# Second attention's output projection in fp16 halves with a power-of-two scale of its own for each chunk, and a new order of the loop

## The reference

```python
def attn_b(x, ...):                       # the second attention
    ...                                   # q, k turned by position, projected to rank 16, gated
    def step(M, inp):
        q_t, k_t, v_t, g_t = inp
        M = M * decay + einsum('bhr,bhd->bhrd', g_t * k_t * scale, v_t)
        y = einsum('bhr,bhrd->bhd', q_t, M)
        return (M, y)
    ...
    out = Y @ out_w.T + out_b             # what this change is about: 512 x 512
    hres = x + out
    ...                                   # layer norm of hres, times ln_g, plus ln_b

x = x + attn_a(layernorm(x), ...)
x = x + ffn(layernorm(x), rhs)
x = x + attn_b(layernorm(x), ...)
x = x + ffn(layernorm(x), rhs)
```

## Time and profile before

| | |
|---|---|
| median of 3 runs | 3149.44 us |
| the profiled execution's own time | 3152.03 us |
| its span, first to last instruction | 3150.2 us |
| TensorE busy | 3027.0 us (96%) |
| VectorE busy | 2457.6 us (78%) |
| GpSimd busy | 1028.1 us (33%) |
| ScalarE busy | 734.0 us (23%) |
| mean granted TensorE clock | 0.983 of full speed |
| DMA | 153.89 MB, 49 GB/s |

### The profile page before, as it was taken

The page is one execution under the profiler, slowest core; times in us unless marked ns, Lnnn a source line. Parts: engine busy times, 40 slices in busy tenths (PEclk is TensorE's granted clock), DMA queues, the critical chain, the costliest instruction groups (busy, mean ns, idle before and its releaser), DMA issues.

```text
span 3150.2 us, 126598 instructions
## 1 busy us (share of the span) xinstructions
PE 3027.0 (96%) x54932; PEld 2288.7 (73%) x54932; DVE 2457.6 (78%) x5410; ACT 734.0 (23%) x1357; POOL 1028.1 (33%) x1398
## 2 busy tenths in 40 slices
PE   3699999999999999999999999999999999999995
PEld 3477777777777777777777777777777777777763
DVE  7777787787787887787787778778778778778774
ACT  2222221222222222222122122222222222222211
POOL 2023333333333333333333333333333333333332
PEclk9799999999999999999999999999999999999997
DMA  5222222222222222222222222222222222222220
GB/s 176 62 40 50 42 45 50 42 45 51 41 45 51 41 49 47 44 47 49 44 48 45 45 47 45 51 41 45 51 41 47 49 42 48 49 46 45 48 41 20
DMA packets 384395, 153.89 MB, mean 49 GB/s; under 512 B 352801, under 2 KB 361633, under 8 KB 383905
## 3 DMA queue, kind: packets, MB, share of 16 engines
q1 hardware_dynamic: 383904, 146.02, 23.4%
HBM read 45.29 MB, written 16.78 MB: 20 GB/s over the span
## 4 chain that ended last, share of the span: by engine, by line
PE 94%; DVE 3%; issue 1%; DMA 1%; ACT 0%; POOL 0%; POOLq 0%; SPq 0%; DVEq 0%; ACTq 0%
PE bank L726 22%; PE bank L727 21%; PE bank L728 21%; PE bank L1020 7%; PE bank L899 3%; PE bank L808 3%; PE bank L852 3%; PE bank L684 3%; PE bank L972 2%; PE bank L871 2%; PE bank L826 2%; PE bank L995 2%; PE bank L982 1%; DVE absmax L1163 1%; PE bank L1008 1%
## 5 line engine op out<-in xcount | busy, mean ns | idle before, releaser
L726 PE MATMUL bank<-xaT,wq_hi 128*128 128x128 f16 x2048 | 362.5, 221 | 4.5 <-DVE absall L1173 4.5
L726 PE MATMUL bank<-xbT,wb 128*128 128x128 f16 x2048 | 350.8, 220 | 13.3 <-DMA xbT<-work 13.3
L727 PE MATMUL bank<-xaT,wq_hi 128*128 128x128 f16 x2048 | 361.1, 221 | 0.0
L728 PE MATMUL bank<-xaT,wq_lo 128*128 128x128 f16 x2048 | 361.0, 221 | 0.0
L726 PE MATMUL bank<-xaT,wk_hi 128*128 128x128 f16 x2048 | 358.5, 220 | 0.0
L727 PE MATMUL bank<-xaT,wk_hi 128*128 128x128 f16 x2048 | 358.4, 220 | 0.0
L728 PE MATMUL bank<-xaT,wk_lo 128*128 128x128 f16 x2048 | 358.4, 220 | 0.0
L727 PE MATMUL bank<-xbT,wb 128*128 128x128 f16 x2048 | 350.8, 220 | 0.0
L728 PE MATMUL bank<-xbT,wb 128*128 128x128 f16 x2048 | 350.7, 220 | 0.0
L646 POOL TENSOR_TENSOR work<-work 128x512 f32<-128x512 f32 x128 | 162.3, 1268 | 421.4 <-DVE work L1418 421.4
L1306 DVE TENSOR_SCALAR work<-bank,eps_q 128x256 f32<-128x256 f32 x256 | 122.9, 480 | 175.8 <-PE bank L728 172.1
(11 more groups left out here) (210 smaller groups left out, 8438.7 us busy)
## 6 DMA issues: line engine op xcount, KB each, us to landing
xin<-in_L_attn_a_x SPq DMA_DIRECT2D x64, 256.0 KB, 2.6
out<-xf SPq DMA_DIRECT2D x64, 256.0 KB, 2.1
table<-in_tables SPq DMA_DIRECT2D x64, 192.5 KB, 2.5
work<-in_L_attn_a_Wq SPq DMA_DIRECT2D x1, 2048.0 KB, 8.2
work<-in_L_attn_a_Wk SPq DMA_DIRECT2D x1, 2048.0 KB, 12.6
wb<-in_L_attn_a_Wv SPq DMA_DIRECT2D x1, 2048.0 KB, 17.3
work<-in_L_attn_a_Wo SPq DMA_DIRECT2D x1, 2048.0 KB, 8.5
work<-work SPq DMA_TRANSPOSE x128, 3.6
```

Of the source, the lines that this page charges most:

```text
L726: nc.tensor.matmul(o, a[0], b[0], start=first, stop=False)
L727: nc.tensor.matmul(o, a[0], b[1], start=False, stop=False)
L728: return nc.tensor.matmul(o, a[1], b[0], start=False, stop=last)
```

## The change

- `out` works on halves. `out_w` is prepared like the other weights, to `wout_hi` and `wout_lo`. For `y` the scale is found anew in each chunk: VectorE's `y_m` takes the largest magnitude of each row of `yT`, TensorE's `y_r` turns these 128 numbers into a row by one transpose (into bank 6, unit `ym`), VectorE's `y_s` takes their maximum and makes from it the power of two and its inverse in four short instructions, ScalarE's `y_h` writes the high half, VectorE's `y_l` the low half, and `out` is 12 fp16 matmuls. `out_e` multiplies by the inverse scale and adds in one instruction.
- The DMA of the fp32 `wout` is gone from the start; `load out` stands in slot 2.
- The table is in another order. Its start, and with it the loop's joint, stands behind `wo1`, where it stood behind `out`. The largest lag is 4, where it was 5, so the first 10 slots are written out and the loop has 27 turns. `LATE`, `BANK` and `COUNTS` follow.
- Waits of one step for several units on the same bank are made one (`all_filled`, `take_behind`).

```diff
-         ("out", 3), ("out_e", 3), ("no_st", 3), ("ld_t", 2), ("ub_a", 3), ("u0_e", 1)]
+         ("qk2_e", 0), ("bias", 1), ("qk3_e", 0), ("nb_st", 2), ("nb_rs", 2), ("aT0_t", 1), ("out", 3),
+         ("u0", 1), ("out_e", 3), ("no_st", 3), ("no_rs", 3), ("u0_e", 1), ("no_ap", 3), ("no_f", 3),
+         ("nb_ap", 2), ("aT1_t", 1), ("wo0", 1), ("xTb_h", 2), ("wo1", 1)]
...
+    def take_behind(self, units, read):
+
+        last = {}
+        for u in units:
+            last[BANK[u]] = max(last.get(BANK[u], (0, -10 ** 9)), self.uses(u), key=lambda n: n[1])
+        for u, back in read:
+            if self.exists(back):
+                per, const = self.uses(u, back)
+                last[BANK[u]] = max(last.get(BANK[u], (0, -10 ** 9)), (per, const + 1), key=lambda n: n[1])
+        for b, n in last.items():
+            self.wait(self.empty[b], n)
+        return [(self.ps[BANK[u]], self.full[BANK[u]]) for u in units]
...
-        wout = sb("wout", [P, KD, D])
+        wout = (sb("wout_hi", [P, KD, D], F16), sb("wout_lo", [P, KD, D], F16))
...
-            sp.dma_start(wout[:, :, :], out_w.rearrange("(k p) n -> p k n", p=P)).then_inc(s_wout, 16)
...
+            def y_r(c):
+
+                bank, f = c.take("ym")
+                c.wait(y_reduced, c.count())
+                nc.tensor.transpose(bank[:, 0:P], y_max[:, :].to_broadcast([P, P]), ident[:, :]).then_inc(f, 1)
+
             def out_(c):
                 bank, f = c.take("out")
-                c.done("y0")
-                c.done("y1")
-                if c.per == 0 and c.j == 0:
-                    pe.wait_ge(s_wout, 16)
+                c.wait(y_halved, c.count())
+                need(c, "out")
                 for k in range(KD):
-                    last = nc.tensor.matmul(bank[:, :], yT[:, k, :], wout[:, k, :], start=k == 0, stop=k == KD - 1)
+                    last = three_pass(bank[:, :], (y_split[:, 0, k, :], y_split[:, 1, k, :]), w_part(wout, k, slice(0, D)),
+                                      k == 0, k == KD - 1)
                 last.then_inc(f, 1)
...
+            def y_h(c):
+                c.wait(y_scaled, c.count())
+                c.filled("sb3")
+                nc.scalar.activation(y_split[:, 0, :, :], yT, ACT.Copy, scale=y_scale[:, :]).then_inc(y_hi, 1)
...
+            def y_m(c):
+                c.done("y0")
+                c.done("y1")
+                nc.vector.tensor_reduce(y_max[:, :], yT.rearrange("p k t -> p (k t)"), AX_X, ALU.max,
+                                        apply_absolute_value=True).then_inc(y_reduced, 1)
+
+            def y_s(c):
+
+                bank, e = c.read("ym")
+                nc.vector.tensor_reduce(y_all[:, :], bank[:, 0:P], AX_X, ALU.max).then_inc(e, 1)
+                c.done("ym")
+                nc.vector.tensor_scalar(y_small[:, :], y_all[:, :], 2.0 ** -80, 2.0 ** -12, ALU.max, ALU.mult)\
+                    .then_inc(y_bounded, 1)
+                c.wait(y_bounded, c.count())
...
+            def y_l(c):
+                c.wait(y_scaled, c.count())
+                c.wait(y_hi, c.count())
+                nc.vector.scalar_tensor_tensor(y_split[:, 1, :, :], yT, y_scale[:, :], y_split[:, 0, :, :], ALU.mult,
+                                               ALU.subtract).then_inc(y_halved, 1)
+
             def out_e(c):
                 bank, e = c.read("out")
                 c.wait(xn_bias, c.count())
-                nc.vector.tensor_tensor(xnb[:, :], bank[:, :], xnb[:, :], ALU.add).then_inc(e, 1)
+                nc.vector.scalar_tensor_tensor(xnb[:, :], bank[:, :], y_unscale[:, c.par:c.par + 1], xnb[:, :],
+                                               ALU.mult, ALU.add).then_inc(e, 1)
```

## The result

The changed kernel takes 3168.4 us (median of 4, 3163.9 to 3172.0) against 3149.9: a ratio of 1.0059, 95% interval 1.0041 to 1.0076. It is slower, by 0.6%; 3116 was forecast, with a range from 3088 to 3148. In the runs further down two executions lie far above the others of their kernel, 3199.3 us in e3_u0 and 13830.0 us in e6_const; the medians count them, the ratios leave them out.

What follows compares the result with a forecast made beforehand. TensorE, busy 96%, was taken as the bound. Terms: -45.8 (`out` less `y_r`), -4 joint, +6 waits, +7 end, +3 start = -33.8 us, from 3152.0 to 3118.2, median 2.6 lower: 3116, range 3088 to 3148.

Steps and rivals of the forecast that it cites:

- `out` itself: Output projection on TensorE: 12 fp16 matmuls take 2.59 us instead of 3.49, gaining 0.90 us a chunk.
- `y_r`: One fp32 transpose of 128 x 128 on TensorE: 0.15 us a chunk, bounds 0.11 and 0.22.
- The waits at `y_r` and `out`: TensorE waiting for `y_m` or `y_l`: 0 to 1.0 us a chunk at `out`, 0.1 taken, 6 us lost.
- two rivals: Waits at `y_r` or `out`: half the gain lost, 3140, chance 0.18; `out`'s saving becomes equal wait, 3156, chance 0.03.
- rival one: Half the gain lost to waits at `y_r` or `out`, 0.5 us a chunk: 3140 us, chance 0.18.
- The rest of the table is packed closer too ... I take 0.1 us a chunk: Allowance for `y_l` being late and the closer order with VectorE at 86%: 6 us lost.
- rival two: VectorE becomes the bound, with 39.5 us of work a chunk and over 7.2 of waits: 3174 us, chance 0.08.
- The joint: Longer chunk behind the loop's joint, 0.39 us a turn, about 10 us in all: 4 us gained.
- The end: Last slots, where no other chunk covers the longer chain from `yb` to `out`: 7 us lost, bounds 0 and 12.
- The start: Preparing `out_w`, at most 6.2 us more on VectorE: 3 us lost, bounds 10 gained and 10 lost.
- the prediction's own signs: Signs of error: steady TensorE wait at L1051 or `out`, interval above 46.4, `y_l` near 2, loop over 10 us later.

Runs made afterwards that it cites:

- e3_u0: Changed kernel with `u0` issued right behind `u1` again instead of behind `out`: 3152.2 us.
- e6_const: Changed kernel with y split at a fixed scale of 1, without `y_m`, `y_r` and `y_s`: 3173.2 us.
- e5_bank: Changed kernel with q's low half ahead of `o1_e`, `qr` in bank 5, `kt0_e` behind `v1_e`, `qb_h` ahead of `gb_s`; `kr_e` left: 3141.9 us.
- e7_all: Changed kernel with rhs and Wk loaded behind chunk 1's x, `u0` behind `u1`, and q's low half ahead of `o1_e`: 3118.5 us.
- e2_oldout: Changed kernel's order, banks and joint with the old output projection of 8 fp32 matmuls, no maximum, scale or halves: 3226.7 us.
- e1_load: Changed kernel with the loads of rhs and Wk issued behind the load of chunk 1's x instead of ahead of it: 3159.6 us.
- e11_pad128: Halves in the before-kernel's order, xa's low half and `qk3`'s eviction earlier, plus 128 empty TensorE instructions ahead of the loop: 3182.6 us.
- e12_before_pad: Kernel before, unchanged but for 90 empty TensorE instructions ahead of its loop: 3266.4 us.
- e8_plain: Halves of `out` put into the order, banks and joint of the kernel before, with `qk3` covering the split: 3288.3 us.
- e9_fetch: Halves in the before-kernel's order, with xa's low half computed right behind q's first eviction so its transpose is issued earlier: 3223.3 us.

## Why the prediction was wrong

**`out` itself: right.** 12 matmuls at 0.216; 2.59 plus 0.09. The gain is 0.81 a chunk instead of 0.90, since the small fp32 tiles of `u0` now follow it.

**`y_r`: near in size.** 0.15 taken, 0.205 measured, inside the bounds: 0.11 for the transpose and 0.09 for the small tiles behind it, which the prediction didn't count.

**The waits at `y_r` and `out`: there are none.** The prediction took 0.1 us a chunk and spent two rivals on them. `y_l` took 0.76, since it starts 0.16 us ahead of the addition that was feared (its argument against rival one), and it is ready 1.07 us early.

**The failed step is the sentence "The rest of the table is packed closer too ... I take 0.1 us a chunk".** It gave one allowance to everything that the order moves, and looked only at the two new meetings with VectorE. Measured are 0.37 at two old meetings (`qr` and `kT`, shown by e5_bank), 0.16 for taking `u0` from `u1` (e3_u0), and 0.26 for other new changes from one kind of matmul to another, less 0.15 gone elsewhere. That is 0.64 against the 0.60 that `out` and `y_r` gain together. e7_all, in which the first two are undone, has 46.01, 0.04 from the prediction's 45.97 (46.72 less 0.75). That it comes so near is partly luck: 0.17 stay at `mm0`, `mm1` and the transposes, and `o` and the last matmul of `qk1` give back 0.2.

**VectorE as the bound** (rival two) did not come: 83% busy in the window. But it had no pause above 0.04 us from 1499.0 to 1518.5, and what TensorE asks for at `qr` and `kT` lies in that stretch. The share over a turn, 79% before, hid this.

**The joint:** 4 us gained were taken. The longer interval exceeds the shorter by 0.26 on average, where it was 0.36. Of the 0.36, only 0.12 was in `s`; 0.24 was in `o`, which took 1.82 us in every second chunk and 1.58 in the others, and takes 1.58 and 1.62 now. The prediction saw the registers gone from the middle of `o`, which no run tests by themselves. That is some 5 us in the run, near the 4 taken, but `s`, with `kt0` behind it, takes 0.10 more in every chunk and uses it up.

**The end:** 7 lost were taken. `y_m`, `y_r` and `y_l` do wait there (11 us in six waits), but the last intervals are shorter otherwise, and 0.3 us is the difference.

**The start:** 3 lost were taken with bounds of 10, 16.9 were measured. The prediction counted the new weight's work on VectorE at 6.2 us at most and held it harmless where TensorE waits anyway; TensorE waited 7.2 us for that weight's maximum alone, and without the weight the first `out` comes 10.5 us earlier (e2_oldout, of it 1.9 for the scale). And it didn't see that a load on SyncE's queue with a wait stands ahead of chunk 1's x, which was in the order to be read: 8.6 us (e1_load).

Of the prediction's own signs two spoke: the interval above 46.4, and the first slot more than 10 us late. The sum by measured terms: the 60 intervals from the first `out` -0.5 (2805.6 against 2806.1), the start +16.9, the end -0.3, against 16.0 in the spans.

## What to carry to other kernels

A change of the order isn't free where the engine has no idle time to show. Compare the step from each unit's last matmul to the next unit's first, before and after: waits shorter than a matmul's modelled duration (0.15 us behind one of 0.38 here) stand in no idle column.

Read the order for the loads too: each entry of a queue that can wait holds up everything behind it.

Before an experiment on a long loop is believed, look for stalls that nothing released. If they are there (0.4 to 1.9 us a chunk here), the instructions' place has its part in the time, and the run says little about the edit.

## What the runs showed of the hardware

**TensorE runs out of instructions.** The rows above (e11, e12) say that the program comes in pieces of 256 instructions. In `so` and `o` it uses 320 of them (160 small matmuls and their weight loads) in 2.7 us. A boundary that fell 51 to 96 instructions behind the start of `so` was followed, at the next boundary, by a stall of 0.7 to 2.2 us in all nine places that had one. Behind one at 35 (the other half of e2_oldout's loop) there were a few short ones (up to 0.48 us), and behind those at 145 to 242 none above 0.3. In e6_const, with one at 2, `o` had short stalls and `qk1` longer ones; the changed kernel's boundary lies 18 instructions earlier and it has no stall. What decides there stays open. A transpose by DMA (1056 packets, 0.26 MB) just ahead of the piece goes with a longer stall: 1.9 us a chunk in e8_plain, 1.2 in e9_fetch, where it is issued earlier. Here is the window 1008.0 to 1012.4 of e12_before_pad, DMA queues and issues:

```profile
q1 hardware_dynamic: 1056, 0.26, 61.2%
q8 instruction: 1, 0.02, 1.3%
...
xaT<-xa_split SPq DMA_TRANSPOSE x1, 4.5
```

**An increment of a semaphore by TensorE costs about 0.15 us** when nothing else is in its row: in e11_pad128 they follow each other at 0.15 us, and TensorE stands idle 17.5 us for 128.

**VectorE and GpSimd.** In the changed kernel (its VectorE rows stand above) the low half of 128 x 512 takes 1.76 us from 1503.90, beside the first of these two GpSimd rows, and 1.05 from 1508.03, beside the second:

```profile
1503.46 1.66 POOL L688 TENSOR_TENSOR work<-work 128x512 f32<-128x512 f32 x1 [1.56 <-DVE work L1454]
...
1507.27 1.26 POOL L683 TENSOR_TENSOR xwb<-xwb,lnb_row 128x512 f32<-128x512 f32 x1
```

In e5_bank the second one takes 0.68, where no addition runs:

```profile
1631.15 1.76 DVE L1449 TENSOR_TENSOR work<-work 128x512 f16<-128x512 f32 x1
...
1633.23 0.68 DVE L1449 TENSOR_TENSOR work<-work 128x512 f16<-128x512 f32 x1
```

Moving it away from its neighbour gave VectorE 0.37 us where it was late. Both times the low half ends 0.5 us behind the addition's end. Where VectorE's instruction starts first (`y_l`, above), it takes 0.74 and the addition takes longer, 1.71 for 1.27. The Trainium skill ("SBUF — State Buffer", section "SBUF: two separate sides") says that a VectorE instruction with two SBUF inputs and a GpSimd instruction that reads SBUF share a pair of ports, and that whichever starts first has it for its whole instruction. These rows agree.

**A change from fp16 matmuls to small fp32 tiles costs 0.09 us** (2.590 against 2.683 for the same twelve matmuls of `out`, e3_u0 and e7_all against the changed kernel).
